# Three CIN layers on one core: X0 turned by two 78-row transposes, one chunk ahead and in the second group

## The reference, cut to what matters

```python
def _cin_layer(X0, Xi, W, b):                 # W: (H, F0*Fi), H = 128
    Wr = W.reshape(H, F0_, Fi)
    return jnp.einsum('hjk,bjd,bkd->bhd', Wr, X0, Xi) + b[None, :, None]
X0 = e                                        # (512, 39, 16)
for W, b in [(W0, b0), (W1, b1), (W2, b2)]:
    Xi = _cin_layer(X0, Xi, W, b)
    res.append(Xi.sum(axis=2))
z = concatenate(res, axis=1)                  # (512, 384)
h = relu(concatenate([z, dense_ctx], axis=1) @ W_top1 + b_top1)
h = relu(h @ W_top2 + b_top2);  y = h @ W_top3
```

## Time and profile before

| | |
|---|---|
| median of 3 runs | 655.04 us |
| profiled execution, its own time | 654.38 us |
| its span, first to last instruction | 652.5 us |
| TensorE (PE) busy | 617.7 us, 95% |
| VectorE (DVE) busy | 581.6 us, 89% |
| ScalarE (ACT) busy | 558.5 us, 86% |
| GpSimd (POOL) busy | 470.9 us, 72% |
| granted TensorE clock | 1.000 (2.4 GHz) |

### The profile page before, as it was taken

One profiled execution on the slowest core, in us unless ns is written; L12 is line 12 of the kernel. 1 busy time (PEld: TensorE's weight loads), 2 busy tenths in 40 slices (PEclk: granted clock), 3 DMA queues, 4 the chain that ended last, 5 costly groups with the idle time before them and its releaser, 6 DMA issues.

```text
span 652.5 us, 14351 instructions
## 1 busy us (share of the span) xinstructions
PE 617.7 (95%) x2595; PEld 477.3 (73%) x2595; DVE 581.6 (89%) x1233; ACT 558.5 (86%) x1767; POOL 470.9 (72%) x442
## 2 busy tenths in 40 slices
PE   0389999999999999999999999999999999999998
PEld 0146788787878787878788787878787878876673
DVE  0549999999999999999999999999999999999980
ACT  3048899999999999999899989999999999999782
POOL 6778898979797989989798979798987656420000
DMA  7533404131222314040414132231405050000200
GB/s 228 135 78 88 125 19 126 34 105 53 79 81 49 109 21 137 9 137 17 126 32 121 39 91 67 67 91 39 120 8 149 1 150 5 12 18 1 65 1 0
DMA packets 44274, 46.16 MB, mean 71 GB/s; under 512 B 20896, under 2 KB 27264, under 8 KB 44233
## 3 DMA queue, kind: packets, MB, share of 16 engines
q1 hardware_dynamic: 38482, 43.59, 23.0%
q0 software_dynamic: 5120, 1.32, 2.4%
q10 hardware_dynamic: 631, 0.74, 0.4%
HBM read 44.30 MB, written 1.31 MB: 70 GB/s over the span
## 4 chain that ended last, share of the span: by engine, by line
PE 88%; issue 4%; DVE 4%; POOL 1%; ACT 1%; DMA 1%; DVEq 0%
PE ya L528 12%; PE ya L530 12%; PE ya L529 12%; PE yd L528 9%; PE yd L530 8%; PE yd L529 8%; PE misc L511 5%; PE acc L500 4%; PE acc L499 3%; PE acc L501 3%; PE acc L504 2%; DVE chain L651 2%; POOL emb L390 1%; PE yd L611 1%; PE yd L609 1%
## 5 line engine op out<-in xcount | busy, mean ns | idle before, releaser
L779 ACT ACTIVATE prods<-ya,x0t 128x128 f32<-128x128 f32 x1472 | 452.0, 519 | 40.8 <-PE ya L530 37.8
L651 DVE SCALAR_TENSOR_TENSOR chain<-yd,x0t,chain 128x128 f32<-128x128 f32 x768 | 218.2, 343 | 4.9 <-remote 4.0
L390 POOL DMA_INDIRECT emb<-in_tables,rows x160 | 158.4, 990 | 35.4 <-issue 24.3
L528 PE MATMUL ya<-w1h,x1h 128*128 128x512 f32 (+1 forms) x384 | 166.4, 433 | 3.2 <-ACT prods L779 2.1
L437 POOL TENSOR_TENSOR prod0l<-prod,prod0h 120x512 fp32r<-120x512 f32 x98 | 127.6, 1302 | 47.8 <-ACT prod0h L788 47.2
L529 PE MATMUL ya<-w1l,x1h 128*128 128x512 f32 (+1 forms) x384 | 147.5, 384 | 0.0
L530 PE MATMUL ya<-w1h,x1l 128*128 128x512 f32 (+1 forms) x384 | 147.2, 383 | 0.0
L305 POOL TENSOR_TENSOR prod<-tiles,x0a 120x512 f32<-120x512 f32 x105 | 137.3, 1308 | 12.5 <-issue 4.2
L666 DVE TENSOR_REDUCE x2t<-prods 128x128 f32<-128x1792 f32 x64 | 129.2, 2019 | 2.4 <-issue 0.3
L666 DVE TENSOR_REDUCE prods<-prods 128x128 f32<-128x1536 f32 x64 | 111.7, 1746 | 0.1
L528 PE MATMUL yd<-w1h,x1h 128*128 128x512 f32 x256 | 102.5, 400 | 1.9 <-DVE prods L651 1.6
(11 more groups left out here) (102 smaller groups left out, 620.9 us busy)
## 6 DMA issues: line engine op xcount, KB each, us to landing
tiles<-x_rows SPq DMA_DIRECT2D x236, 78.0 KB
x0a<-x_rows SPq DMA_DIRECT2D x45, 80.0 KB
emb<-in_tables,rows POOLq DMA_INDIRECT x160
w<-in_w SPq DMA_DIRECT2D x3, 832.0 KB, 5.6
w<-in_w SPq DMA_DIRECT2D x13, 192.0 KB
tiles<-x_rows SPq DMA_DIRECT2D x32, 42.0 KB
x<-x_rows SPq DMA_DIRECT2D x16, 78.0 KB
x<-x_rows SPq DMA_DIRECT2D x16, 77.8 KB
```

What stands on the lines that cost most here:

```text
L390: pool.indirect_dma_start(emb[:, c % 2, fo * D:(fo + 1) * D], None, a["tables"], bass.IndirectOffsetOnAxis(ap=rows[:, c, fo:fo + 1].bitcas ...
L528: pe.matmul(out, x1h[:, c % 2, xs], w1h[:, cols], start=True, stop=False)
L651: dve.scalar_tensor_tensor(out, product, x, run if step else b1[:, :], ALU.mult, ALU.add).then_inc(yd_used, 1)
L779: mm = act.activation(prods[:, :, slot_of(q) + i], ya[(NA * g + k) % YA][:, i * H:(i + 1) * H], ACT.Copy, scale=turned(c)[:, g * F1 + j:g ...
```

## The change

X0 is loaded twice (`XB = 2`) in place of three times, so the tile `x0` has 78 rows, and both transposes take 78 rows: the first turns groups 0 and 1, the second, at column offset 2, groups 2 and 3. The columns turned are 156 as before. The transposes of chunk c + 1 are done in chunk c after (1, 1), in place of those of chunk c + 2 after (3, 1), for every chunk but the last; chunk 0's exception goes. ScalarE's copy moves with them to after (1, 2) (written as q = 3). ScalarE rounds product 0 of chunk c + 2 after (3, 7) in place of (3, 4), ahead of the copy of the Gram product.

```diff
-XB = 3
+XB = 2
-G_AFTER, TURN_1 = 6, (0, 8)
+G_AFTER, TURN_AFTER = 6, (1, 1)
-HIGH_AFTER = {0: (3, 4), 1: (0, 0), ...}
+HIGH_AFTER = {0: (3, 7), 1: (0, 0), ...}
-def turn_after(prev):
-    return (3, 1)
                 pe.transpose(misc[:, 0:XB * F], by_group[:, 0, :], const[0:XB * F, C_ID:C_ID + XB * F])
-                pe.transpose(misc[:, XB * F:GROUPS * F], by_group[0:F, XB, :], const[0:F, C_ID:C_ID + F]
+                pe.transpose(misc[:, XB * F:2 * XB * F], by_group[:, XB, :], const[0:XB * F, C_ID:C_ID + XB * F]
# TensorE
-                        if not prev and (g, q) == TURN_1:
-                            pe.wait_ge(x0_ready, 2)
-                            turn_x0(1)
+                        if nxt and (g, q) == TURN_AFTER:
+                            pe.wait_ge(x0_ready, c + 2)
+                            wait_done(pe, g_ready, GROUPS * c + g - 1)
+                            turn_x0(c + 1)
-                        if lay and (g, q) == turn_after(prev):
-                            pe.wait_ge(x0_ready, c + 3)
-                            wait_done(pe, g_ready, GROUPS * c + g - 1)
-                            turn_x0(c + 2)
                         if q == G_AFTER and (g or prev):
-                            if not prev and g == 1:
-                                pe.wait_ge(x0t_ready, 2)
+                            if nxt and g == TURN_AFTER[0]:
+                                pe.wait_ge(x0t_ready, c + 2)
-                            if lay and g == turn_after(prev)[0]:
-                                pe.wait_ge(x0t_ready, c + 3)
# ScalarE
-                        if lay and (g, q - 2) == turn_after(prev):
-                            evacuate_x0t(c + 2)
-                        if not prev and (g, q) == (TURN_1[0], TURN_1[1] + 1):
-                            evacuate_x0t(1)
+                        if nxt and (g, q - 2) == TURN_AFTER:
+                            evacuate_x0t(c + 1)
```

More of the change, by code:

```diff
@@ L83 @@
 SPLIT, SPLIT_FROM = tuple(range(T0)), 2
-HIGH_AFTER = {0: (3, 4), 1: (0, 0), 2: (0, 5), 3: (1, 0), 4: (1, 5), 5: (2, 0), 6: (2, 5)}
+HIGH_AFTER = {0: (3, 7), 1: (0, 0), 2: (0, 5), 3: (1, 0), 4: (1, 5), 5: (2, 0), 6: (2, 5)}
 assert sum(GATHERS_AFTER) == FO
```

## The result

The changed kernel takes 659.46 us (median of 5 runs, 656.66 to 660.6), the kernel before 655.04 on the same chip: a ratio of 1.0061, 95% interval 1.0032 to 1.0089, or 4.0 us slower by the ratio (2.1 to 5.8 by the interval; 4.4 between the medians). The forecast was 3.1 us slower, with 657.0 to 659.3 us for its own mechanism; the median lies 0.2 us above that band.

What follows compares the result with a forecast made beforehand. VectorE, not TensorE, was taken to set when (0, 3) starts, with TensorE setting the stretch from there to (2, 1). 14 x 0.25 = 3.5, less 0.25, less 0.15, made 3.1 us slower: 658.1 us, range 655.3 to 662.4.

Steps and rivals of the forecast that it cites:

- what TensorE is spared in the last group turns into waiting: Last group: removing the transposes saves TensorE 0.54 us, but its wait for VectorE at (0, 3) grows by as much.
- The new place is on the path, 14 times: After (1, 1), chunks 1 to 14: VectorE waits for TensorE there, nothing hides the transposes; 14 x 0.25 = 3.5 us slower.
- T = 0.25: Cost in us of the X0 transpose pair in its new 78-row form, 0.54 before; bounds 0.13 and 0.54.
- The waits of the earlier trace: TensorE's weight loads for yd wait 8.2 us in 15 times, nearly all at (0, 3) of chunks 2 to 15.
- stretch V: From (2, 1) to the next (0, 3), where VectorE was said to work without a gap, 17.9 us.
- the period of chunk 14: Chunk 14, without lay_out and X0 transposes, still takes 35.13 us; taken as a trial that VectorE sets (0, 3).
- VectorE's idle at (2, 1) from 0.60 to 0.85: Start of the third group: sign that VectorE's idle, released by TensorE, grows from 0.60 to about 0.85 us.
- The rounding is free: Product 0's rounding three blocks later: cost 0, cover 1.4 us; GpSimd's wait there grows from 0.51 to about 1.8 us.
- TensorE as the bound of every stretch: Rival: the place is free and the shape saves 4.6 us, giving 650.4 us, faster; chance 0.06.
- a shape that saves nothing: Rival: the pair still costs 0.54 us at the new place, 7.5 less 0.4 slower, 662.1 us; chance 0.16.
- the larger gain at the start: Rival: one load less shrinks ScalarE's standstill at the start by up to 2.1 us, giving 656.0 us; chance 0.12.
- The start gives 0.15, chunk 0 another 0.25: Gains: 0.15 us from one x0 load less at the start, 0.25 at (0, 3) of chunk 1, which had no wait.

Runs made afterwards that it cites:

- e1: Kernel before with only the new shape (two loads, two 78-row transposes), old place and rounding: ratio 0.9990, 655.17 us against 655.42.
- e2: Kernel before with only the new place (after (1, 1)), old shape of 117 and 39 rows, old rounding: ratio 1.0134, 663.72 us against 655.42.
- e9: Changed kernel with three loads and transposes of 117 and 78 rows: ratio 1.0040 to the kernel before, 659.17 us against 656.11.
- e4: Changed kernel with VectorE's sum over dimensions moved from third to second group in chunks 1 to 14: ratio 1.0057 to the kernel before, 658.64 us.
- e3: Kernel before with only product 0's rounding moved from (3, 4) to after (3, 7): ratio 1.0009, 655.25 us against 655.42.
- e5: Kernel before with new shape at old place, rounding after (3, 7), x1's low part on GpSimd: ratio 0.9864, 641.19 us against 650.18.
- e8: Changed kernel with old shape (117 and 39 rows, three loads) and x1's low part on GpSimd: ratio 0.9958 to the kernel before, 646.86 us.

## Why the prediction was right, point by point

- *VectorE sets the start of (0, 3), and what TensorE is spared in the last group turns into waiting.* Right, shown by e1.
- *The new place is on the path, 14 times.* Right, shown by e2 (0.54 a chunk); in the changed kernel 0.27 a chunk by the period, 0.25 forecast. Averaged over chunks 2 to 13, the stretch from (0, 3) to (2, 1) grew from 17.24 to 17.53 us, and that from (2, 1) to the next (0, 3) stayed (17.88, now 17.87): all that was added lies where the forecast put it.
- *T = 0.25.* Measured 0.24, and 0.24 again with 195 columns (e9), which fits the sum's reading that two weight loads make it up and not the columns. The period grew by 0.03 more than that; why, I did not find.
- *The waits of the earlier trace rows.* Read too widely: of the 8.2 us, 5.7 lie at (0, 3) in 11 places, 0.97 in chunk 0 and three times 0.51 in the tail. The sum does not use it.
- *The end points of stretch V.* Wrong in one: it begins at (3, 1), not at (2, 1), as e4 showed. I took "no idle before the last group" for "VectorE alone decides", when both engines arrive together. The sum was not touched, since the old place of the transposes lies within the true stretch, and the period of chunk 14 fits either reading.
- *VectorE's idle at (2, 1) from 0.60 to 0.85.* Wrong in place: it is still 0.58 in chunk 14 (559.14), but 0.19 us of idle appeared at its block (1, 6), which the later TensorE now delays (the profile names VectorE's own chain, but that had ended, and TensorE starts the last pass of this block only at 553.95):

```profile
554.57 1.12 DVE L641 SCALAR_TENSOR_TENSOR chain<-yd,x0t,chain 128x128 f32<-128x128 f32 x4 [0.19 <-DVE chain L641]
...
559.14 0.35 DVE L641 SCALAR_TENSOR_TENSOR chain<-yd,x0t,b 128x128 f32<-128x128 f32 x1 [0.58 <-PE yd L525]
```

- *The rounding is free.* Right (e3). GpSimd's wait there is 2.12 us (504.38) in the changed kernel, 1.8 forecast, and its total 54.6, 7 more, where up to 15 were allowed.
- *The rivals.* TensorE as the bound of every stretch fell by e1; a shape that saves nothing fell by the pair's 0.24 us and by e2 against the changed kernel; the larger gain at the start, 2.1 us, has no sign in the time.
- *The start gives 0.15, chunk 0 another 0.25.* Neither is shown. The first block did start 1.21 us sooner (37.99 for 39.20), but over all eleven traces it starts between 36.74 (e2, three loads) and 39.37 (e5, two loads), so this is not the load less. And (0, 3) of chunk 1 came at 81.30, where the earlier trace rows has 80.36: 0.94 later in this execution. What was won was waited out: matmuls of blocks (1, 1) and (1, 2) in chunk 0,

```profile
49.93 0.74 PE L523 MATMUL yd<-w1h,x1h 128*128 128x512 f32 x1 [4.34 <-DVE chain L641]
50.47 0.63 PE L524 MATMUL yd<-w1l,x1h 128*128 128x512 f32 x1
```

and VectorE ahead of them had stood still since 42.1:

```profile
48.75 1.13 DVE L641 SCALAR_TENSOR_TENSOR chain<-yd,x0t,chain 128x128 f32<-128x128 f32 x4 [6.62 <-remote]
```

In the kernel before, VectorE stands still at this point too, for 4.03 us, and the earlier trace rows has TensorE's wait of 2.13. The two executions differ in more than the kernel: the one profiled before had a mean clock of 1.000, as 4 of 29 of its runs have on the chip of e1 to e4 (last section), the changed one 0.997. Of kernels level with before, e3 has (0, 3) of chunk 1 at 80.30 in an execution at 1.000, and e1 has it at 81.91 in one at 0.995. So the 0.94 is no price of the change. The periods make 3.8 of the 4.0 us, which leaves some 0.2 for start and tail together, where the sum had 0.40 off for them; the interval of 2.1 to 5.8 us is too wide to call these terms right or wrong. What VectorE waits for in its standstill stays open.

## What to carry to other kernels

When two engines share a loop through a pair of buffers, ask for each stretch of the loop which one waits at its end; work moved from where an engine arrives early to where another waits for it costs its full length, whatever the busy shares and the chain say. A free trial can stand in the trace: a first or last round that lacks the piece (here chunk 14, less work and the same period). And "no idle" before a piece doesn't say who decides; here only taking work from one engine told it (e4).

## What the runs showed that I had not expected

After the 4.34 us idle of TensorE at the start, the granted clock fell, and the steps of 512 columns went from 0.23 to 0.42 us. Windows of the changed kernel (in us: length, busy of PE, PEld, DVE, ACT and POOL, then the clock, the DMA share and GB/s):

```profile
48.00:52.00 4.00, 2.07 (x6) 1.68 (x7) 3.25 (x8) 2.43 (x9) 2.81 (x3) 0.75 0.56 150
52.00:56.00 4.00, 4.00 (x14) 2.71 (x13) 4.00 (x10) 2.70 (x11) 0.96 (x1) 0.82 0.30 85
```

0.75 and 0.82 are a mix of its two levels, 1.2 and 2.4 GHz; in the kernel before, with an idle of 2.13 us, the clock stayed at 1.00, and so it did in e3 with 2.18. The runs of the kernel before point the same way: on the chip of e1 to e4, 25 of 29 had a mean clock of 0.995 or 0.997 (654.24 to 657.01 us), four had 1.000 (651.74 to 654.07), so a part of the spread of some 5 us between runs seems to be made in this start.

On the chip of e5 to e8 it looks otherwise. None of the four traces has VectorE's standstill: from 40 to 56 us TensorE has no wait of 1 us or more, and the clock stays at 1.00. The kernel before had 1.000 there in all 11 runs, and 650.18 us in place of 655. It has no trace on that chip, so that the missing standstill makes these 5 us is likely but not shown; the comparison of e5 to e8 with it does not hang on that, since their periods give 8.4 of the 8.8 us of e5.
